# The expert ring of a two-layer transformer: who waits for the weights, where TensorE loads its addresses, and where the first weight units land

## The reference

```
layer 0: 16 experts of width 256, 4 of them per token, and one shared expert for all tokens
layer 1:  8 experts of width 1024, 2 of them per token
h1 = x w1^T;  h3 = x w3^T;  h = silu(h1) * h3;  y = sum over chosen experts of weight * (h w2^T)
x = x + y   (layer 0: + z, the shared expert's output)
```

## Time and profile before

| | |
|---|---|
| Median of 3 runs | 2456.65 us (2449.45 to 4039.03) |
| Profiled execution, its own time | 2449.88 us |
| Its span | 2448.1 us |
| Busy: PE, DVE, ACT, POOL | 1884.8, 912.4, 616.4, 790.4 us |
| Mean granted clock of TensorE | 0.887 of full |

### The profile page before, as it was taken

How to read it: one execution, slowest core, us unless ns; L and a number is a source line. 1 busy time by engine, 2 the same in 40 slices (tenths; PEclk the granted TensorE clock), 3 DMA queues, 4 the chain that set the end, 5 groups by cost and what they waited for, 6 DMA issues and landing times. The chain is left out here.

```text
span 2448.1 us, 44368 instructions
## 1 busy us (share of the span) xinstructions
PE 1884.8 (77%) x15646; PEld 1556.9 (64%) x15646; DVE 912.4 (37%) x2100; ACT 616.4 (25%) x1360; POOL 790.4 (32%) x540
## 2 busy tenths in 40 slices
PE   6768899337777775399999999787715888989893
PEld 5436777226666664278888888665514777777773
DVE  5443625543222231613333333345543333333333
ACT  2111515212121220223333333343522111111110
POOL 0003421144546104233333333221020884818102
PEclk9988999669999996699999999867867999999997
DMA  6750010663435215211111110100063443414103
GB/s 228 275 199 22 18 52 1 237 247 125 155 132 178 70 61 147 96 27 36 35 34 34 34 34 26 40 5 23 29 230 112 153 162 100 155 58 139 39 14 112
DMA packets 97191, 237.08 MB, mean 97 GB/s; under 512 B 9712, under 2 KB 26736, under 8 KB 97040
## 3 DMA queue, kind: packets, MB, share of 16 engines
q1 hardware_dynamic: 68768, 172.84, 20.5%
q10 hardware_dynamic: 20592, 36.98, 4.5%
q0 software_dynamic: 7680, 25.17, 3.1%
HBM read 183.58 MB, written 51.38 MB: 96 GB/s over the span
## 5 line engine op out<-in xcount | busy, mean ns | idle before, releaser
L128 PE MATMUL banks<-weights_F,rest_r_F 128*128 x920 | 325.7, 354 | 61.8 <-issue 32.6
L128 PE MATMUL banks<-ra_DE 128*128 128x258 f32 (+2 forms) x912 | 321.3, 353 | 30.5 <-ACT fa_DE L2007 8.5
L129 PE MATMUL banks<-ra_DE 128*128 128x258 f32 (+2 forms) x912 | 311.9, 343 | 0.0
L130 PE MATMUL banks<-ra_DE 128*128 128x258 f32 (+2 forms) x912 | 310.9, 342 | 0.0
L129 PE MATMUL banks<-weights_F,rest_r_F 128*128 x920 | 287.4, 312 | 0.0
L130 PE MATMUL banks<-weights_F,rest_r_F 128*128 x920 | 286.6, 312 | 0.0
L128 PE MATMUL banks<-weights_C,rest_r_C 128*128 (+1 forms) x486 | 186.1, 383 | 108.6 <-issue 80.3
L128 PEld LDWEIGHTS banks<-weights_F,rest_r_F 128*128 128x128 f32 x920 | 182.0, 198 | 112.8 <-issue 106.1
L128 PEld LDWEIGHTS banks<-ra_DE 128*128 128x128 f32 (+1 forms) x912 | 177.5, 195 | 63.3 <-ACT fa_DE L2007 14.3
L128 PEld LDWEIGHTS banks<-weights_C,rest_r_C 128*128 128x128 f32 x486 | 100.0, 206 | 148.1 <-issue 144.6
L130 PEld LDWEIGHTS banks<-ra_DE 128*128 128x128 f32 (+1 forms) x912 | 178.5, 196 | 19.3
(11 more groups left out here) (458 smaller groups left out, 3643.5 us busy)
## 6 DMA issues: line engine op xcount, KB each, us to landing
rest_F<-in_L_units SPq DMA_DIRECT2D x64, 768.0 KB, 4.3
rest_C<-in_L_units SPq DMA_DIRECT2D x36, 768.0 KB
fa_DE<-in_ctxT SPq DMA_DIRECT2D x32, 514.0 KB, 3.9
e_sorted<-temps_C SPq DMA_DIRECT2D x1, 12032.0 KB, 38.0
rest_C<-e_sorted ACTq DMA_DIRECT2D x47, 256.0 KB, 2.7
ea_y_scratch<-rest_C ACTq DMA_DIRECT2D x47, 256.0 KB, 2.4
fa_AB<-in_ctxT SPq DMA_DIRECT2D x16, 514.0 KB, 8.6
fa_cross<-in_ctxT SPq DMA_DIRECT2D x16, 514.0 KB, 8.3
```

What stands on the lines that cost most here:

```text
L128: pe.matmul(psum, lh, rh, start=first, stop=False)
L129: pe.matmul(psum, lh, rl, start=False, stop=False)
L130: return pe.matmul(psum, ll, rh, start=False, stop=last)
```

## The change

1. **ScalarE hands on the counts.** TensorE no longer loads `count` nor waits for `s_split`. ScalarE loads it (L1618), waits, and raises a new semaphore `s_ready` (L1622) right after it has issued the silu of the unit before; `up` of unit n waits for `s_ready` of n + 1.
2. **Address loads elsewhere.** TensorE's offset loads (L1792) stand behind `down` of the unit in the middle of the tile, one behind each of two units in F (the fourth and fifth of eight), one behind the first of two in C.
3. **Split of `up`.** One triple of the next unit stands ahead of `turn_h`, and three behind it.
4. **The first units straight into the ring.** The first R routed-side units are loaded into the low half of their own slot (memory `tails` that shares the ring's place), each with its own semaphore, with no wait for staging; the low part is then written over the raw numbers.
5. **The start.** The number of the expert per rank is announced as soon as it is known, and SyncE starts its loads then; the rest of the tables has a second count. In C, ScalarE waits for tables and scatter only before the first routed tile's rows, in the fourth shared tile; the routed units 2 to 7 are split during units 3 to 8. In F only 6 of the 12 units are split before the first rows are loaded, the other 6 one by one behind the silus of the first 6 units.

```diff
+                self.preloaded = self.first * U
                 self.s_ld = [sem(f"e{layer}_loaded{b}") for b in range(S_)]
+                self.s_fill = [sem(f"e{layer}_filled{n}") for n in range(self.preloaded, self.slots)]
...
+            def place(self, n):
+                e, q = divmod(n, self.units)
+                return (e * self.offsets + q // self.group) % self.groups * self.group * UNIT + q % self.group * UNIT
+            def raw(self, n):
+                if n < self.preloaded:
+                    return self.staging[n], self.s_ld[n], 16
+                if n < self.slots:
+                    return tails[self.place(n) // UNIT][:, 3 * D:UNIT], self.s_fill[n - self.preloaded], 16
+                b, k = (n - self.slots) % self.staged, (n - self.slots) // self.staged
+                return self.staging[b], self.s_ld[b], 16 * (k + 1 + (b < self.preloaded))
             def load_unit(self, eng, w, n, expert):
-                b = n % self.staged
-                eng.dma_start(self.staging[b], w[expert * self.units + n % self.units]).then_inc(self.s_ld[b], 16)
+                dst, s_landed, _ = self.raw(n)
+                eng.dma_start(dst, w[expert * self.units + n % self.units]).then_inc(s_landed, 16)
...
+            START, SHIFT = (U, -1) if plan.shared else (6, 6)
+            s_ready = sem(f"{tag}_weights_ready")
...
-                    for n in range(plan.first * U, units):
+                    for n in range(plan.preloaded, units):
                         r = n // U - plan.first
                         if n % U == 0 and r < E:
                             e = eng.value_load(plan.expert.bitcast(U32)[0:1, r:r + 1], min_val=0, max_val=E - 1)
-                        if n >= STAGED:
+                        if n >= R + STAGED:
                             eng.wait_ge(s_split, n - STAGED + 1)
+                        elif n >= R and n - R < plan.preloaded:
+                            eng.wait_ge(s_split, n - R + 1)
                         plan.load_unit(eng, w, n, e if r < E else E)
...
+                    def count(i):
+                        kind, j = tiles[i]
+                        if kind == "shared":
+                            return U * (0 if j < FIRST_TILES else plan.ranks - 1)
+                        return eng.value_load(plan.count.bitcast(U32)[0:1, j:j + 1], min_val=0, max_val=U * (plan.ranks - 1))
+                    def ready(q, needed):
+                        eng.wait_ge(s_split, needed + (q + 1))
+                        eng.sem_inc(s_ready, 1)
+                    def first_rows():
+                        eng.wait_ge(s_tables, 2)
+                        eng.wait_ge(plan.s_scattered, 16 * K * NT)
+                        load_rows(0)
+                        load_rows(1)
                     act.activation(table[:, 0:1], epst[:], ACT.Silu)
-                    start = 2 if plan.shared else R
-                    for n in range(start):
+                    for n in range(START):
                         weights_high(n)
-                    eng.wait_ge(s_tables, 1)
-                    eng.wait_ge(plan.s_scattered, 16 * K * NT)
-                    load_rows(0)
-                    load_rows(1)
                     if not plan.shared:
+                        first_rows()
                         rows_high(0)
+                    needed = count(0)
+                    ready(0, needed)
...
                             act.activation(sg[q % 2], banks[:, HB + q % 2, 0:P], ACT.Silu).then_inc(s_sg, 1)
+                            if q < U - 1:
+                                ready(q + 1, needed)
+                            elif i + 1 < TILES:
+                                ready(0, ahead)
+                            if START <= n + SHIFT < R:
+                                weights_high(n + SHIFT)
                             if q == U - 2 and i + 1 < TILES and tiles[i + 1][0] == "routed":
+                                if plan.shared and tiles[i + 1][1] == 0:
+                                    first_rows()
                                 rows_high(tiles[i + 1][1])
                             if q == 0 and i:
                                 keep_y(i - 1)
-                            weights_high(n + start)
+                            if q == U - 2 and i + 1 < TILES:
+                                ahead = count(i + 1)
+                        needed = ahead
...
                         links.link(dve.tensor_copy(plan.expert.bitcast(U32), some))
+                        eng.sem_inc(s_tables, 1)
...
-                                self.count = U * e
                                 self.at = [(e * plan.offsets + h) % plan.groups * plan.group * UNIT for h in range(plan.offsets)]
                             else:
-                                self.count = eng.value_load(plan.count.bitcast(U32)[0:1, j:j + 1], min_val=0,
-                                                            max_val=U * (plan.ranks - 1))
-                                self.at = [eng.value_load(plan.offset.bitcast(U32)[0:1, h, j:j + 1], min_val=0,
-                                                          max_val=(plan.groups - 1) * plan.group * UNIT)
-                                           for h in range(plan.offsets)]
+                                self.at, self.tile = [], j
+                        def load(self):
+                            if len(self.at) < plan.offsets:
+                                self.at.append(eng.value_load(plan.offset.bitcast(U32)[0:1, len(self.at), self.tile:self.tile + 1],
+                                                              min_val=0, max_val=(plan.groups - 1) * plan.group * UNIT))
...
-                            eng.wait_ge(s_split, wt.count + (q + 1))
-                            eng.sem_inc(s_began, 1)
+                            eng.wait_ge(s_ready, n + 1)
...
-                                if i + 1 == FIRST_TILES:
-                                    eng.wait_ge(s_tables, 1)
-                                ahead = Weights(i + 1)
...
-                                up(*following, range(0, 2))
+                                up(*following, range(0, 1))
                             turn_h(U * i + q, q)
                             if following:
-                                up(*following, range(2, DC))
+                                up(*following, range(1, DC))
                             down(i, q, wt)
+                            if i + 1 < TILES:
+                                if q == 0:
+                                    ahead = Weights(i + 1)
+                                if q in range(U // 2 - 1, U // 2 - 1 + plan.offsets):
+                                    if i + 1 == FIRST_TILES:
+                                        eng.wait_ge(s_tables, 2)
+                                    ahead.load()
...
+                    tails = [area(f"tail{n}", [P, UNIT]) for n in range(plan.slots)]
```

More of the change, by code:

```diff
@@ L1470, in experts @@
             for g in free:
-                a = Area(tail, R * UNIT, g * plan.group * UNIT)
-                yt += [a.take(D) for _ in range(plan.group * UNIT // D)]
+                for slot in range(g * plan.group, (g + 1) * plan.group):
+                    a = Area(tails[slot], UNIT)
+                    yt += [a.take(D) for _ in range(UNIT // D)]
             yt = yt[:K * NT]
@@ L1476, in ring @@
             def ring(n):
-                e, q = divmod(n, U)
-                at = (e * plan.offsets + q // plan.group) % plan.groups * plan.group * UNIT + q % plan.group * UNIT
+                at = plan.place(n)
                 return weights[:, at:at + 3 * D], weights[:, at + 3 * D:at + UNIT]
@@ L1545, in _ @@
                         hi, lo = ring(n)
-                        eng.wait_ge(plan.s_ld[n % STAGED], 16 * (n // STAGED + 1))
+                        raw, s_landed, count = plan.raw(n)
+                        eng.wait_ge(s_landed, count)
                         if plan.shared and e == 0:
@@ L1555, in _ @@
                         eng.sem_inc(s_began, 1)
-                        pool.tensor_copy(hi, plan.staging[n % STAGED]).then_inc(s_pair, 1)
+                        pool.tensor_copy(hi, raw).then_inc(s_pair, 1)
                         eng.wait_ge(s_pair, n - R + 1)
-                        pool.tensor_tensor(lo, plan.staging[n % STAGED], hi.bitcast(F32), ALU.subtract).then_inc(s_split, 1)
+                        pool.tensor_tensor(lo, raw, hi.bitcast(F32), ALU.subtract).then_inc(s_split, 1)
                     wait_stored(eng)
@@ L1568, in weights_high @@
                         if n < R:
-                            eng.wait_ge(plan.s_ld[n % STAGED], 16 * (n // STAGED + 1))
-                            act.activation(ring(n)[0], plan.staging[n % STAGED], ACT.Copy).then_inc(s_hi, 1)
+                            raw, s_landed, count = plan.raw(n)
+                            eng.wait_ge(s_landed, count)
+                            act.activation(ring(n)[0], raw, ACT.Copy).then_inc(s_hi, 1)
```

(14 more changed lines are left out.)

1 line of the change is left out of this document (removed).

## The result

The kernel after takes 2253.81 us (median of 4 runs, 2253.08 to 2262.02) against 2454.3 us of the kernel before (median of 4, 2449.45 to 4039.03): a ratio of 0.9197, 95% interval 0.9165 to 0.9228. The one run of 4039.03 us stands outside the ratio, and nothing here explains it. I had said 2270, range 2205 to 2345. The profiled execution has a span of 2252.5 us, 195.6 less than before.

The account below looks back on a forecast made before the run. Parts C and F were taken to be bound by TensorE's products and the gaps between them. Terms of 53, 15, 31, 18, 12, 14, 27, 11 and 2 us sum to 183 off 2449.9, 2267; forecast 2270 us, range 2205 to 2345.

Parts of the forecast that it names:

- The unit: Units within F and C tiles: three products behind `turn_h` cover `down`'s wait, 0.33 us per unit; 53 us F, 15 C.
- the 0.2 us of slack: Units: `turn_h`, coming earlier, still finds silu and multiply done, 0.92 us against 1.16 after the last `up` product.
- One load fewer in C: End of C's tiles: one register load less saves 0.65 us per tile, 31 us; fewer clock drops give 14 more.
- F's loads and clock: F's tiles: two places with one load each instead of three together, 18 us; no clock drops, 12 us.
- The count on ScalarE: ScalarE's `ready` word and count load cost nothing, with 0.2 us per unit as upper bound.
- F's start: Start of F: earlier weight loads and fewer first splits bring TensorE's start 31 to 32 us earlier; net 27 us.
- of 387 GB/s 179 are left for weights: F's start: the scatter takes 208 GB/s, so weights arrive at 4.4 us per 786 KB unit.
- C's start: Start of C: shared tiles run before the scatter ends, first routed `turn` 14 us earlier; net 11 us.
- The allowance of 15 us either way: C's end: VectorE, ScalarE and TensorE stand still, once 16.9 us, while GpSimd gathers; unexplained, allowed 15 us either way.
- Gaps did not stay: Rival for tiles of C and F: load gaps and clock drops remain, about 100 us gained, 2350 us; chance 0.20.
- the word was not late: Rival: `up` waits for ScalarE's word, 0.2 us in each of 290 units, 58 us, 2328 us; chance 0.10.
- The loads vanish: Rival at tile ends: TensorE's queue runs ahead and covers one load, another 55 us off, 2215 us; chance 0.13.

Follow-up runs that it names:

- the undone split: Kernel after with two of the four quarters of `up` ahead of `turn_h` again and two behind: 2289.34 us, ratio 0.9456.
- the first eight experiments: Both kernels unchanged, and six one-edit variants of the kernel after, up to C's gathers held back the first time; before took 2421 to 2422 us there.
- the three edits undone: Kernel after with one undone each: split of `up` 2289.34 us, ScalarE's hand-over of counts 2290.87, address loads in two places (together again) 2226.13.
- the held loads: Kernel after, but in F SyncE issues six unit loads beside the scatter and waits for its end before the seventh: 2208.37 us, ratio 0.9119.
- the last four runs: Kernel after with C's gathers held again (2244.05 us), address loads ahead of `down` (2223.38), h split ahead of rows and count load moved (2196.58), three gains combined (2165.57).

## Why the prediction held, step by step

- **The unit** (53 and 15 us): right in mechanism and size. 50.5 in 22 F tiles and 15.0 in C, from the undone split. `turn_h` starts at most 0.13 us behind the product ahead of it in 177 of F's 184 units, so the 0.2 us of slack held.
- **One load fewer in C** (31, with 14 of clock 45): the mechanism was right, the term too small. The step that failed priced the place at 2.19 - 0.65 us, as if only a load went. The 0.65 of a load holds, but the register sum and increment of TensorE's wait went with it, and I had put them at nothing: 0.25 us more, 0.91 in all, 42 us. The clock gave about 13. Together 55.4 measured, and with the split's 15.0 this is 70.4 of the 72.0 us that C's tiles gained on the chips of the first eight experiments. The longer first load of C was not what I missed: it is still there, 0.55 in the median.
- **F's loads and clock** (18 and 12): the load term was too small for the same reason. 20.0 for the load with the wait's register sum, 7.4 for the two places: 27.4 against 18, without any part of the clock. The full clock in F came as said, but it stays full with any one of the three edits undone (1.00 from 1850 to 2042 us), so these runs don't show its 12 us. F's 22 tiles gained 84.8 in all on the chips of the first experiments; the three edits' parts are 77.9 of them, and the other 6.9 I put down to the clock, unproven. From the last turn to the end F gained 5.7 us, where I had counted the 2.3 of one tile's units. A lone load sticks out 0.23 us in the trace (2151.96 to 2152.89, against 0.70), half of what I had taken.
- **The count on ScalarE** (nothing): right. In four of F's eight units `up` follows `down` by 0.70 us, as without a wait. In the other four something else stands there: a load in two, the next tile's turn in one (1.05), and in one a `down` that had waited for VectorE (0.80).
- **F's start** (31 at the first product): 23.5 at the turn. The step "of 387 GB/s 179 are left for weights" was the wrong way round. With 14 loads queued the weights took 786 KB per 2.96 us (the second and the fifth unit's copies start at 1727.94 and 1736.81), 265 of 422 GB/s, and the scatter, which is issued at 208, got the rest. Its end, not the sixth unit, then ends the wait; the held loads gave 8.0 back. No run undid the early loads, the loads straight into the ring or the smaller first split by itself, so what each of them gave is open, and so are the 4 us I took back for the late splits.
- **C's start** (14): 13.6 on chips without standstills, 5.4 on the one of the comparison. The allowance of 15 us either way, made for the unexplained standstill at C's end, covered it.
- **The rivals.** Gaps did not stay, the word was not late. "The loads vanish" was right in a part: in F half of what I let stand vanished, in C 0.46 us instead of 0.74 stands behind `down`. My mark for C's tiles, 6.5 us, was not what my own terms give (7.95 - 57 / 46 = 6.7); 6.32 was measured.

The errors partly cancel: 18 us too little for C's tiles and 13 for F's, about 8 too much for each start. So the total, 13 off in the gain, is better than its terms, and that is luck: the two kinds of error have different causes.

## What to carry to other kernels

A register load costs what sticks out behind the products that are queued when it is issued: put it ahead of the instruction that waits, not behind it. When you price taking it away, count every sequencer step between the last product and the next (here the register sum and increment of a wait, 0.25 us beside 0.65), since behind a load nothing hides them. An early transfer can starve the one on the path: issue only as many loads as the first consumer needs. In an engine's own order, what feeds TensorE next goes first, and what feeds it later behind that (VectorE's split of h ahead of the rows).

## What the hardware showed

- On some chips TensorE's words reach ScalarE and VectorE late, by 9 to 27 us (a product at 508.07, its silu at 517.76; at C's end products done at 868.4 and the silu at 895.26), while GpSimd's indirect DMAs run; on others the same program shows nothing of it. It showed in the profiles of before and of after and in the last four runs, and in none of the other eight. Words between other engines were on time in the same stretch (ScalarE's silu at 517.76, VectorE's multiply at 518.07). What holds TensorE's words, and what sets the chips apart, stays open.
- A register load of TensorE takes 0.30 us in F, in the median of every place, also directly behind a `down` that had waited (median of 46 in the run with the loads in one place). In C one directly behind such a `down` takes 0.56 in the median and up to 1.3; ahead of it, behind another load or behind a `down` that had not waited it takes 0.30. Why C differs was not found.
